# Building a graph's count matrix on TensorE: the register values of each step group moved from one row on partition 0 to a partition of their own

## The chip, the core and the metric

The kernel is one program on one core of a Trainium2 chip. Its time is the device time of that core in microseconds (us). TensorE (PE) multiplies, VectorE (DVE) and ScalarE (ACT) work on vectors, GpSimd (POOL) fills buffers and gathers, SyncE (SP) issues the plain DMAs here. Each engine has a sequencer of its own that also holds registers; a TENSOR_LOAD copies values of a tensor in the on-chip memory (SBUF, 128 partitions) into such registers, where they can be used as addresses.

## The reference

Four graph layers run one after the other on x (3125 nodes, 128 features), over the same 103,125 edges (`src`, `dst`, sorted by `dst`). The first two layers need plain sums over neighbours:

```python
edge_index = jnp.stack([src, dst])
h = jnp.maximum(_layernorm(x, axis=-1), 0.0)
x = x + _L0_gnn_ref(h, edge_index, ...)        # aggr = segment_sum(h[src], dst); batch norm
h = jnp.maximum(_layernorm(x, axis=-1), 0.0)
x = x + _L1_gnn_ref(h, ..., src, dst)          # two rounds of segment_sum(h[src], dst) / degree
h = jnp.maximum(_layernorm(x, axis=-1), 0.0)
x = x + _L2_gnn_ref(h, edge_index, ...)        # attention over the edges
h = jnp.maximum(_layernorm(x, axis=-1), 0.0)
x = x + _L3_gnn_ref(h, ..., edge_index, edge_type_8)   # a weight for each of 8 edge types, two rounds
return x
```

The change touches no number of this. It lies in a stage that prepares the three neighbour sums of the first two layers.

## The kernel before

**The count matrix.** The three sums are matrix products with a matrix that tells how often node s is a source of node d. The kernel builds it on the chip, in blocks of 4 target nodes: `CELLS` = 100 columns are one block (25 source tiles times 4 targets). The edges come in `STEPS` = 1596 steps, each 128 edges against one block. A step is one matmul (L670): a one-hot matrix of the low digit of `src` (`hot_lo`) times a one-hot matrix of the cell (`hot_cell`), added into the block's 100 columns in PSUM (`sums`).

**Epochs and windows.** 19 steps (`STEPS_OF`) form an epoch, of which there are 84 (`EPOCHS`). Two halves of PSUM take turns, one for each epoch. Four epochs form a window (21 of them), a buffer `filled[w % 2]` of 7700 columns (the trace calls it `adj_window`). Four engines work at each epoch, each in its own written order:

- DVE, `compare_epochs`: L647 writes `hot_lo`, L649 writes `hot_cell`; it may be one epoch ahead of TensorE (`estep_n`).
- TensorE, `count_edges`: L658 loads 20 registers (`SLOTS`), the places of the 19 steps in PSUM and one carry; L666 opens four banks with four matmuls of zeros; L670 is the 19 steps; L675 adds the columns that the last epoch left open; L679 closes the banks.
- ACT, `move_out`: L697 moves the half into the window buffer at a place that comes from a register (L685 loads four of them for a window).
- SP, `store_windows`: L704 loads one register, and L708 stores the whole window to DRAM (`adj`), 128 partitions of 30,800 bytes. It waits until the window's four epochs are moved out, and for the store before it.

**What a register load reads.** The values stand in `steprow`, [1, 84, 32] int32: all on partition 0, epoch e in 20 words from word 32 e. DVE makes them in L371 to L388; the mark of the last of these is `stepped`. All other loads of the program read partition 0 as well: `windowrow` (L704), `epochrow` (L685), `d0row` (L1066, 13 values), `pairrow` (L1194, 13), `pair_place` (L1386, 11 values from word 0, 11 and 22), `offrow` (L575, 13).

**The order around it.** TensorE's instructions run in the order in which they are written. Before its first load TensorE turns four weight matrices (L403) and waits for ACT to have taken them (L406). SP has issued the loads of the inputs and three stores of tables (L301 to L303) before the stage, and then waits for `stepped`. `mark` pairs such as `stepped` are a semaphore and the count to wait for; `Dma.did` adds 16 to its semaphore when a DMA has landed.

Of the kernel before, what the change touches and what calls it, by code (L numbers as in the profile page):

```python
# [6 lines left out]
I32 = mybir.dt.int32  # L7
# [5 lines left out]
ENG = mybir.EngineType  # L13
# [31 lines left out]
CELLS = HI * WD  # L45
KT = 7
STEPS_OF = 19
SLOTS = STEPS_OF + 1
EPOCHS = 84
# [4 lines left out]
SPANNED = GROUP * STEPS_OF + 1  # L54
# [54 lines left out]
def build(nc, a, out):  # L109
    with ExitStack() as ctx:  # L110
        def sem(name):
            return ctx.enter_context(nc.semaphore(name))
# [5 lines left out]
        A = Lane(nc.scalar, sem("s_act"))  # L118
        T = Lane(nc.tensor, sem("s_pe"))
# [83 lines left out]
        def tmp(stack, name, shape, dt=F32):  # L203
            return stack.enter_context(nc.sbuf_tensor(name, shape, dt))
# [5 lines left out]
        steprow = tmp(dense, "steprow", [1, EPOCHS, 32], I32)  # L210
# [163 lines left out]
        for q in (2, 3):  # L374
# [13 lines left out]
        stepped = V.did(V.after().tensor_tensor(carry[:, 1:WINDOWS, 0], b0w[:, 1:WINDOWS, 0], b0w[:, 0:WINDOWS - 1, 0],  # L388
                                                ALU.subtract))
# [243 lines left out]
        build = ExitStack()  # L633
# [8 lines left out]
        def compare_epochs():  # L642
            V.after()
            for e in range(EPOCHS):
                if e > 1:
                    nc.vector.wait_ge(estep_n, e - 1)
                nc.vector.tensor_tensor(hot_lo[e % 2][:, :, :], iota_lo[:, :, :],  # L647
                                        los[:, e, :].unsqueeze(1).to_broadcast([P, P, STEPS_OF]), ALU.is_equal)
                nc.vector.tensor_tensor(hot_cell[e % 2][:, :, :],  # L649
                                        iota_cell[:, :].unsqueeze(1).to_broadcast([P, STEPS_OF, CELLS]),  # L650
                                        cells[:, e, :].unsqueeze(2).to_broadcast([P, STEPS_OF, CELLS]),
                                        ALU.is_equal).then_inc(ehot_n, 1)

        def count_edges():
            T.need(stepped, A.now())
            for e in range(EPOCHS):
                half = sums[:, (e % 2) * 2048:(e % 2 + 1) * 2048]
                place = nc.values_load_multi_w_load_instructions(  # L658
                    steprow[0:1, e, 0:SLOTS], engines=(ENG.PE,), min_val=0, max_val=(SPANNED - 1) * CELLS,
                    skip_runtime_bounds_check_because="made on the chip from counts")[1]  # L660
                place = [nc.s_assert_within(v, 0, 2048 - CELLS, skip_runtime_bounds_check_because="made on the chip")
                         for v in place[:STEPS_OF]] + [place[STEPS_OF]]
                if e > 1:
                    nc.tensor.wait_ge(eout_n, e - 1)
                for j in range(4):
                    nc.tensor.matmul(half[:, j * 512:j * 512 + SLOTS // 4 * CELLS], zeros[:, 0:P],  # L666
                                     zeros[:, 0:SLOTS // 4 * CELLS], start=True, stop=False)
                nc.tensor.wait_ge(ehot_n, e + 1)
                for k in range(STEPS_OF):
                    m = nc.tensor.matmul(half[:, bass.ds(place[k], CELLS)], hot_lo[e % 2][:, :, k], hot_cell[e % 2][:, k, :],  # L670
                                         start=False, stop=False)
                m.then_inc(estep_n, 1)
                if e:
                    nc.tensor.wait_ge(eout_n, e)
                    nc.tensor.matmul(half[:, 0:CELLS], ident[:, :],  # L675
                                     filled[(e - 1) // GROUP % 2][:, bass.ds(place[STEPS_OF], CELLS)],
                                     start=False, stop=False)
                for j in range(4):
                    m = nc.tensor.matmul(half[:, j * 512:j * 512 + 1], zeros[:, 0:P], zeros[:, 0:1], start=False, stop=True)  # L679
                m.then_inc(ebuilt_n, 1)  # L680
# [20 lines left out]
        def store_windows():  # L701
            nc.sync.wait_ge(*stepped)
            for w in range(WINDOWS):
# [3 lines left out]
                    nc.sync.wait_ge(s_adj, 16 * w)  # L707
                nc.sync.dma_start(adj[:, bass.ds(first, SPANNED * CELLS)], filled[w % 2][:, :]).then_inc(s_adj, 16)  # L708

        compare_epochs()  # L710
        count_edges()
        move_out()
        store_windows()
# [848 lines left out]
```

## Time and profile before

| | |
|---|---|
| median of 3 runs | 5118.82 us (5105.4 to 5121.59) |
| the profiled execution | 5124.63 us, its span 5123.3 us |
| TensorE busy (matmuls) | 2855.5 us, 56% |
| VectorE busy | 1971.1 us, 38% |
| ScalarE busy | 677.7 us, 13% |
| GpSimd busy | 2395.5 us, 47% |
| the stage that the change touches | 84.0 to 503.6 us of the span |

The shares of busy time are means over stages that differ much: the build of the count matrix is the first tenth, the attention runs from about 1040 to 2600 us, and the rest is the last layer. The profile does not count register loads as busy time: where TensorE's sequencer is in one, the matmul array shows as idle and the wait is put down to "issue". How long each load took is seen when its line is asked for.

### The profile page before, as it was taken

How to read it: one execution, taken by the hardware profiler on the slowest of the kernel's cores; microseconds unless marked ns; L12 is line 12 of the kernel's file. 1: busy time of each engine (PE TensorE's matmuls, PEld its weight loads, DVE VectorE, ACT ScalarE, POOL GpSimd, SP SyncE). 2: the span in 40 equal slices, each digit the busy share in tenths (PEclk: the TensorE clock that was granted, in tenths of full speed). 3: DMA queues.
4: the chain of work that ended last, by engine and by line, in shares of the span. 5: the costliest groups of instructions: out<-in, count | busy, mean ns of one | idle time of the engine just before them, and what ended most of it. 6: DMA issues, size and time to landing. Idle time of an engine off the chain costs nothing.

```text
span 5123.3 us, 41736 instructions
## 1 busy us (share of the span) xinstructions
PE 2855.5 (56%) x12033; PEld 2017.8 (39%) x12033; DVE 1971.1 (38%) x3965; ACT 677.7 (13%) x1897; POOL 2395.5 (47%) x2466
## 2 busy tenths in 40 slices
PE   4666889946666656656626444444346444444343
PEld 3555445534444444444523333333333333333333
DVE  7676765655555555555562111111112111111111
ACT  2334010012222222222311000000001000000000
POOL 3000000055545555555313666666663666666665
PEclk8787989967777777777757555555557555555555
DMA  3444735444333443343304111111114111111111
GB/s 117 201 190 209 306 151 224 188 126 118 109 110 107 118 112 109 114 114 109 85 2 132 47 47 45 46 46 47 46 48 127 46 47 46 47 48 46 46 46 49
DMA packets 294311, 508.93 MB, mean 99 GB/s; under 512 B 68232, under 2 KB 239610, under 8 KB 288968
## 3 DMA queue, kind: packets, MB, share of 16 engines
q1 hardware_dynamic: 216304, 344.29, 18.9%
q0 software_dynamic: 77792, 161.98, 11.4%
q8 instruction: 110, 1.80, 0.1%
q14 instruction: 105, 0.86, 0.1%
HBM read 389.30 MB, written 116.74 MB: 99 GB/s over the span
## 4 chain that ended last, share of the span: by engine, by line
PE 37%; another core or an unknown queue 23%; issue 20%; DVE 6%; POOL 5%; ACT 5%; DMA 2%; ACTq 0%; DVEq 0%; SPq 0%; POOLq 0%
PE sums L587 9%; PE sums L748 8%; POOL edge_buffers L559 5%; PE sums L1105 3%; PE sums L1163 3%; PE sums L1108 3%; ACT trio L1185 3%; PE sums L670 3%; DVE edge_buffers L570 2%; PE sums L1119 2%; PE sums L666 2%; DMA edge_buffers<-rel_t,relidx 2%; PE sums L1477 2%; ACT adj_window L697 1%
## 5 line engine op out<-in xcount | busy, mean ns | idle before, releaser
L559 POOL DMA_INDIRECT edge_buffers<-rel_t,relidx x1612 | 1530.0, 949 | 888.1 <-issue 368.4
L587 PE MATMUL sums<-edge_buffers 128*128 128x128 f32 x3224 | 963.4, 432 | 1332.2 <-issue 1000.8
L587 PEld LDWEIGHTS sums<-edge_buffers 128*128 128x128 f32 x3224 | 748.0, 308 | 1548.9 <-issue 1547.3
L1061 POOL DMA_INDIRECT round_buffers<-xs_t,srcs x806 | 801.5, 994 | 1008.0 <-DVE round_buffers L1240 454.2
L570 DVE TENSOR_SCALAR edge_buffers<-iota,rel 128x128 f32<-128x128 f32 x1612 | 335.5, 300 | 1961.0 <-remote 1506.3
L1163 PE MATMUL sums<-round_buffers 128*128 128x128 f32 x1612 | 282.1, 321 | 441.5 <-ACT trio L1185 363.7
L1163 PEld LDWEIGHTS sums<-round_buffers 128*128 128x128 f32 x1612 | 236.1, 221 | 475.1 <-ACT trio L1185 390.5
L748 PE MATMUL sums<-adj_chunk,H 128*128 128x448 f32 x1050 | 400.2, 542 | 15.6 <-issue 14.4
L1231 DVE TENSOR_TENSOR positive<-positive,sums 128x384 f32<-128x384 f32 x310 | 154.2, 497 | 539.4 <-ACT positive L1175 504.8
L1108 PEld LDWEIGHTS sums<-round_buffers 128*128 128x128 f32 x1612 | 298.0, 238 | 99.5 <-issue 84.2
L1105 PE MATMUL sums<-round_buffers,ident 128*128 128x408 f32 x620 | 317.0, 601 | 28.9 <-DVE trio L1292 24.9
L613 ACT ACTIVATE trio<-sums,c_L_b 128x128 f32<-128x128 f32 x16 | 6.6, 412 | 2312.0 <-PE sums L543 2312.0
L1185 ACT ACTIVATE trio<-sums 128x128 f32 x806 | 225.8, 280 | 589.5 <-remote 319.3
L1108 PE MATMUL sums<-round_buffers 128*128 128x136 f32 x1612 | 296.7, 327 | 0.0
L893 POOL IOTA trio<- 128x806 int32 x1 | 0.8, 805 | 613.0 <-ACT H L502 613.0
L748 PEld LDWEIGHTS sums<-adj_chunk,H 128*128 128x128 f32 x1050 | 200.1, 191 | 210.4 <-issue 208.6
L697 ACT ACTIVATE adj_window<-sums 128x2000 f32 x84 | 154.4, 1838 | 265.3 <-PE sums L679 258.5
L666 PE MATMUL sums<-zeros 128*128 128x500 f16 x336 | 112.6, 470 | 131.8 <-issue 125.8
L649 DVE TENSOR_TENSOR hot_cell<-iota_cell,edge_cell 128x1900 f16<-128x1900 f16 x84 | 178.9, 2130 | 0.0
L1105 PEld LDWEIGHTS sums<-round_buffers,ident 128*128 128x128 f32 x620 | 124.7, 248 | 122.7 <-issue 116.0
L647 DVE TENSOR_TENSOR hot_lo<-iota_lo,edge_lo 128x2432 f16<-128x2432 f16 x84 | 125.3, 1491 | 118.3 <-PE sums L670 118.2
L1234 DVE TENSOR_REDUCE logits<-positive 128x24 f32<-128x384 f32 x310 | 155.3, 501 | 10.7
(273 smaller groups left out, 2683.4 us busy)
## 6 DMA issues: line engine op xcount, KB each, us to landing
adj_chunk<-adj SPq DMA_DIRECT2D x19, 5600.0 KB, 15.9
adj<-adj_window SPq DMA_DIRECT2D x21, 3850.0 KB, 11.2
round_buffers<-xd_t SPq DMA_DIRECT2D x806, 68.0 KB
round_buffers<-rel_tile SPq DMA_DIRECT2D x62, 832.0 KB
edge_buffers<-rel_t,relidx POOLq DMA_INDIRECT x1612
rel_t<-edge_buffers SPq DMA_DIRECT2D x50, 512.0 KB, 3.8
round_buffers<-xs_t,srcs POOLq DMA_INDIRECT x806
round_flags<-seg_tile SPq DMA_DIRECT2D x62, 26.0 KB
```

Source lines behind the costliest of these rows:

```text
L559: nc.gpsimd.indirect_dma_start(slot(t), None, table[:, :], bass.IndirectOffsetOnAxis(ap=index[:, t:t + 1], axis=0)).then_inc(slot_sem(t), 16)
L570: made = nc.vector.tensor_scalar(round_hots(i)[:, k, :], iota[:, :], rel[:, t:t + 1], None, ALU.is_equal)
L587: nc.tensor.matmul(sums[:, bass.ds(place[k], P)], slot(t), round_hots(i)[:, k, :], start=False, stop=False).then_inc(summed_n, 1)
L649: nc.vector.tensor_tensor(hot_cell[e % 2][:, :, :], iota_cell[:, :].unsqueeze(1).to_broadcast([P, STEPS_OF, CELLS]), cells[:, e, :].unsque ...
L666: nc.tensor.matmul(half[:, j * 512:j * 512 + SLOTS // 4 * CELLS], zeros[:, 0:P], zeros[:, 0:SLOTS // 4 * CELLS], start=True, stop=False)
L697: nc.scalar.activation(filled[w % 2][:, bass.ds(at[g], SLOTS * CELLS)].rearrange("p (a c) -> p a c", a=4), bank[:, (e % 2) * 4:(e % 2) * 4 ...
L748: m = nc.tensor.matmul(ps.rearrange("p (b w) -> p b w", w=WD), tables[:, hi, :], held[b][:, :, hi, :], start=(hi == 0), stop=(hi == HI - 1))
L1061: nc.gpsimd.indirect_dma_start(rows[r % RING][:, k * RW:(k + 1) * RW], None, xs_t[:, :], bass.IndirectOffsetOnAxis(ap=srcs[:, t:t + 1], ax ...
L1105: nc.tensor.matmul(pb[2 + q % 2][:, 0:(hi - lo) * RW], ident[:, :], rows[r % RING][:, lo * RW:hi * RW], start=True, stop=False)
L1108: m = nc.tensor.matmul(pb[2 + q % 2][:, (k - lo) * RW:(k - lo + 1) * RW], hotT[:, k * P:(k + 1) * P], win[r % 2][:, k * RW:(k + 1) * RW], ...
L1163: m = nc.tensor.matmul(pb[6 + q % 2][:, (k - lo) * P:(k - lo + 1) * P], msg[:, k * P:(k + 1) * P], hot[r % 2][:, k * P:(k + 1) * P], start ...
L1185: nc.scalar.activation(pairs[:, bass.ds(at[k], P)], pb[6 + q % 2][:, (k - lo) * P:(k - lo + 1) * P], ACT.Copy).then_inc(out_n, 1)
```

## The change

A second tensor `steps_of_epoch` of [84, 20] int32 is allocated, with epoch e's 20 values on partition e. One DMA on SP's queue copies the 84 rows from partition 0 to the 84 partitions; SP waits for `stepped` before it. TensorE's first load waits for that DMA in place of `stepped`, and each L658 reads partition e of the new tensor. In the built program each row of the new tensor begins at byte 228,416 of its partition, and row e of `steprow` at byte 137,248 + 128 e; both are multiples of 16.

```diff
         def count_edges():
-            T.need(stepped, A.now())
+            T.need(s_steps.now(), A.now())
             for e in range(EPOCHS):
                 half = sums[:, (e % 2) * 2048:(e % 2 + 1) * 2048]
                 place = nc.values_load_multi_w_load_instructions(
-                    steprow[0:1, e, 0:SLOTS], engines=(ENG.PE,), min_val=0, max_val=(SPANNED - 1) * CELLS,
+                    steps_of_epoch[e:e + 1, :], engines=(ENG.PE,), min_val=0, max_val=(SPANNED - 1) * CELLS,
                     skip_runtime_bounds_check_because="made on the chip from counts")[1]
...
+        steps_of_epoch = tmp(build, "steps_of_epoch", [EPOCHS, SLOTS], I32)
+        s_steps = Dma(sem("s_steps_turned"))
+        nc.sync.wait_ge(*stepped)
+        s_steps.did(nc.sync.dma_start(steps_of_epoch[:, :], steprow[0:1, :, 0:SLOTS]))
         compare_epochs()
         count_edges()
         move_out()
```

On TensorE at the start of the stage (L403 turns the weights, L658 is the first epoch's load, L666 opens the banks), the order before is this:

```order
L403 MATMUL sums<-ident,trio 128x128 [waits s_dve,s_par,s_pool]
L403 MATMUL sums<-ident,trio 128x128 x3
L658 TENSOR_LOAD steprow [waits s_act,s_dve]
L666 MATMUL sums<-zeros 128x500 x4
L670 ISA [waits s_epoch_hots]
```

and now:

```order
L403 MATMUL sums<-ident,trio 128x128 [waits s_dve,s_par,s_pool]
L403 MATMUL sums<-ident,trio 128x128 x3
L658 TENSOR_LOAD steps_of_epoch [waits s_act,s_steps_turned]
L666 MATMUL sums<-zeros 128x500 x4
L670 ISA [waits s_epoch_hots]
```

Nothing moved: the load stands at its place with another source and another semaphore. The same holds for the 83 loads after it.

On SP between the stores of tables (L302, L303) and the first window (L704), with + for what is added (L713 is the new DMA's line in the changed kernel):

```order
 L302 DMA seg_tile<-trio 128x7x128
 L303 DMA seg_tile<-trio 128x7x384
+L713 DMA steps_of_epoch<-steprow 84x1x20
 L704 TENSOR_LOAD windowrow
 L704 ISA x2
```

One DMA stands ahead of the first window's register load; the rest of SP's order is as it was.

## Rows read from the trace of the kernel before

**Rows 1.** Windows: length; busy of PE, PEld, DVE, ACT, POOL; PEclk, DMA share, GB/s.

```profile
84.00:503.60 419.60, 285.98 (x2434) 221.78 (x2434) 299.83 (x198) 154.51 (x85) 12.93 (x2) 0.80 0.45 189
503.60:5123.30 4619.70, 2540.43 (x9455) 1780.60 (x9455) 1609.30 (x3709) 513.33 (x1801) 2353.30 (x2440) 0.66 0.29 91
```

**Rows 2.** Line L658: duration in ns, min/median/max, then its first and last start.

```profile
L658 PEldq TENSOR_LOAD <-steprow x84: 1356/1372/4841, 84.0 to 496.8; - x84
```

**Rows 3.** The same line in 84:104, 104:111, 111:116, 116:124, 484.5:499.

```profile
L658 PEldq TENSOR_LOAD <-steprow x5: 1359/1367/1553, 84.0 to 100.7; - x5
...
L658 PEldq TENSOR_LOAD <-steprow x1: 4361/4361/4361, 104.5 to 104.5; - x1
...
L658 PEldq TENSOR_LOAD <-steprow x1: 2414/2414/2414, 111.7 to 111.7; - x1
...
L658 PEldq TENSOR_LOAD <-steprow x2: 1356/1356/1357, 116.7 to 120.7; - x2
...
L658 PEldq TENSOR_LOAD <-steprow x3: 1361/2267/4363, 484.9 to 496.8; - x3
```

**Rows 4.** Timeline of PE after the first store began: start, length, what, idle before.

```profile
104.79 0.24 PE L679 MATMUL sums<-zeros 128*128 128x1 f16 x4
108.94 1.82 PE L666 MATMUL sums<-zeros 128*128 128x500 f16 x4 [3.90 <-issue]
```

**Rows 5.** Windows between the starts of the loads of epochs 5 to 9.

```profile
104.56:111.74 7.18, 3.28 (x26) 2.16 (x26) 3.54 (x2) 1.84 (x1) 0.00 (x0) 0.68 0.97 412
111.74:116.74 5.00, 3.77 (x30) 2.65 (x28) 3.54 (x2) 1.84 (x1) 0.00 (x0) 0.50 0.25 102
116.74:120.75 4.01, 3.81 (x41) 3.31 (x38) 3.15 (x2) 1.84 (x1) 0.00 (x0) 0.92 0.00 0
120.75:124.70 3.95, 3.04 (x31) 2.44 (x30) 3.84 (x3) 1.84 (x1) 0.00 (x0) 1.00 0.29 125
```

**Rows 6.** DMA in 103:113.4 us, packets and the store's time to landing.

```profile
DMA packets 128, 3.94 MB, mean 379 GB/s; under 512 B 0, under 2 KB 0, under 8 KB 0
...
adj<-adj_window SPq DMA_DIRECT2D x1, 3850.0 KB, 11.3
```

**Rows 7.** Windows: three slices of the store, columns as in rows 1.

```profile
104.30:105.45 1.15, 0.73 (x9) 0.64 (x8) 0.85 (x2) 0.25 (x1) 0.00 (x0) 1.00 1.01 429
...
110.05:111.20 1.15, 1.15 (x10) 0.81 (x9) 0.00 (x0) 0.00 (x0) 0.00 (x0) 0.50 1.00 429
111.20:112.35 1.15, 1.15 (x15) 1.15 (x14) 0.00 (x0) 0.00 (x0) 0.00 (x0) 0.50 1.07 455
```

**Rows 8.** Other register loads, each line over the whole span.

```profile
L704 SPq TENSOR_LOAD <-windowrow x21: 262/273/712, 63.2 to 483.9; - x21
...
L575 PEldq TENSOR_LOAD <-offrow x124: 1092/1102/3470, 2742.8 to 5086.1; - x124
...
L1066 SPq TENSOR_LOAD <-d0row x62: 1181/1193/1246, 1037.2 to 2500.9; - x62
...
L1194 ACTq TENSOR_LOAD <-pairrow x62: 996/1013/1112, 1096.2 to 2553.2; - x62
...
L1386 PEldq TENSOR_LOAD <-pair_place x3: 1332/2647/2648, 2590.8 to 2620.2; - x3
```

**Rows 9.** Timeline of DVE, and L704 in 60:70 us, around the new DMA's place.

```profile
62.95 0.18 DVE L388 TENSOR_TENSOR steprow<-epoch_block 1x20 int32<-1x20 f32 x1
...
L704 SPq TENSOR_LOAD <-windowrow x1: 481/481/481, 63.2 to 63.2; - x1
```

**Rows 10.** DMA in 0:90 us: small issues, KB each, us to landing.

```profile
rel<-in_dst_col SPq DMA_DIRECT2D x1, 403.0 KB, 7.6
...
c_L_b_rel<-in_L_gnn_b_rel SPq DMA_DIRECT2D x1, 0.5 KB, 3.5
```

**Rows 11.** The two DVE lines of the stage.

```profile
L647 DVE TENSOR_TENSOR hot_lo<-iota_lo,edge_lo x84: 1480/1493/1496, 81.8 to 492.7; 128x2432 f16<-128x2432 f16 x84
...
L649 DVE TENSOR_TENSOR hot_cell<-iota_cell,edge_cell x84: 2127/2130/2134, 83.2 to 494.2; 128x1900 f16<-128x1900 f16 x84
```

## The prediction

> **What bounds the kernel now.** I read the windows first: the change can act only between 84.0 and 503.6 us, 419.6 us of the span; what comes after starts when the stage is done, so what is won or lost there goes into the end time one for one [rows 1]. Neither DVE (299.8 us busy of 419.6) nor ACT (154.5) fills the stage. Next the load line itself: 84 loads of 20 registers, median 1.372 us, but up to 4.841 [rows 2]. Asked for in slices it shows a pattern with a period of four epochs: about 1.36 us as a rule, 4.361 us for the load at 104.5, 2.414 us for the next, then 1.356 again [rows 3]. It repeats in each of the 20 windows that have a store beside them, down to the last, with 4.363 and 2.267 us: 40 of the 84 loads are over 1.6 us. The reader is to see that this is exactly when SP's store of a window is under way: it is issued at 103.4 and its 128 packets, 3.94 MB, land 11.3 us later [rows 6].
>
> The loads lie on the path. In the first slow one TensorE's array ends its work at about 105.0 and idles 3.90 us with the reason "issue" [rows 4]. The distances between four successive loads are 7.18, 5.00, 4.01 and 3.95 us [rows 5]; the first two exceed the last two by about 3.2 and 1.0 us, as their loads do by 3.00 and 1.06. So the sequencer of TensorE sets the pace: the load, then about 2.6 us of everything else. The clock does not enter: 5.00 - 2.41 = 2.59 us at a granted clock of 0.50 (the level of 1.2 GHz), and 3.95 - 1.36 = 2.59 at 1.00. DVE is close behind, with 1.493 + 2.130 = 3.62 us an epoch [rows 11], which is still under the shortest distance.
>
> **What the change could take away.** The excess of one window's loads over the quiet value is (4.361 - 1.357) + (2.414 - 1.357) = 4.06 us; times 20 windows it is 81 us [rows 3]. That is the whole prize, 1.6% of the kernel. Whether it is won hangs on one question: is it partition 0 that is slow to answer during a store, or any partition?
>
> The store treats all partitions alike: 128 packets, one for each partition's 30,800 bytes (3850 KB / 128), and no others [rows 6]. It moves 429 to 455 GB/s with the DMA engines busy all the time, in the first eighth as in the seventh [rows 7]. With 16 engines that is 27 GB/s each and 1.15 us a packet, so an engine has 8 packets in 9.2 us. Partition 0's own packet is thus in motion for one eighth of the store. But the load at 104.5 is slow for all of its 4.36 us, and the one at 111.7, in the seventh and eighth eighth, is slow again. What is busy for partition 0 is therefore not its own row; it is something that it shares with at least the eight rows of one engine, or with all 128. Since all 16 engines are busy to the end, each other partition shares an equally busy thing.
>
> The Trainium skill, "SBUF — State Buffer", section "Door 1: The DMA port swizzle", gives this a shape: 16 ports for the DMA side, each with eight partitions (0 to 3 and 32 to 35 on the first), and a transfer over 128 partitions reaches all of them. By that rule this change spreads the loads over ports that the same store fills alike, and the gain is nothing; by the opposite reading it would be the 81 us above. No row tells which partitions an engine serves; that the rate stays at 27 GB/s an engine agrees with the rule.
>
> I take the gain as 0. Its bounds are 0 (nothing of the wait goes) and -81 us (all goes).
>
> **What the load itself costs on another partition.** No row shows a load from any partition but 0, so I bound it by the other loads [rows 8]. 13 values take 1.102 us on TensorE, 20 take 1.357 (rows 3), one value on SP takes 0.273. This is no price for each value: 1.102 / 4 = 0.276 and 1.357 / 5 = 0.271 fit if up to four values that start at a multiple of four words go together (13 = 3 fours and 1, 20 = 5 fours). The 11 values of `pair_place` fit as well: from word 0 they take 1.332 us (2 fours and 3 singles, 0.266 each), from words 11 and 22 they take 2.647, 11 singles of 0.241. The new rows begin at a multiple of 16 bytes, so they remain 5 requests of 0.271. What may differ is the way to the partition. The same partition 0 costs ACT 1.013 / 4 = 0.253 and SP 1.193 / 4 = 0.298 a request: places of requesters differ by 0.045 us. If places of partitions differ as much, the 84 x 5 = 420 requests cost between -19 and +19 us; I take 0, since the epochs go through 84 partitions and near and far should cancel.
>
> During a store a request costs 4.361 / 5 = 0.872 us. About 7 requests in a window meet it (5 and some 2 of the next load), 140 in all; a difference of 0.06 us either way between partitions is 8 us, inside the same bounds.
>
> **What the change adds.** One DMA of 84 rows of 80 bytes on SP. Its source is ready at 63.1, when DVE's last write ends, and SP is idle there: its next instruction starts at 63.2 [rows 9]. The nearest small DMA lands after 3.5 us, the slowest of the first 90 us after 7.6 [rows 10]; so the rows are there at 67 to 72 us. TensorE does not ask before 84.0 [rows 2], when ACT has let it go. Cover of 12 us or more, cost 0; with the cover gone it would be at most 7.6 us once. Behind it on SP stands the first window's register load, delayed by the issue, about 0.4 us; the store that needs it comes at 103.4. Nobody waits. DVE, ACT and POOL have the same instructions as before, and the loads' count and place on TensorE are unchanged.
>
> **The sum.** 0 (wait) + 0 (price of a request) + 0 (the DMA) on the profiled execution's 5124.6 us. That one lies 5.8 us above the median of the runs, 5118.8; what is compared are medians, so I forecast 5119 us.
>
> **The rivals.**
>
> First, the wait belongs to partition 0. Then all 84 loads take 1.36 us, the windows last 4 x 4.0 us in place of 20.1, and the kernel takes 5119 - 81 = 5038 us. DVE's 3.62 us an epoch would not stop it, and a store (11.3 us) still fits into a window of 16 us. For it: every slow load in the trace does read partition 0, SP's too (0.712 against 0.273) and the last layer's (3.470 against 1.102) [rows 8], so nothing measured speaks for another partition. Against it: the argument of the eighths. A half of it is possible: partitions whose engine's share is done earlier, or which are reached past a less busy place, would bring 20 to 40 us, 5080 to 5099.
>
> Second, the other side: partitions away from 0 answer later. The mechanism is the trip of each request, 420 times in series. It decides from 15.4 / 420 = 0.037 us a request on; at the spread of 0.045 that the requesters show it is +19 us, 5138. A worse form is that the loads fall apart into single values, as from `pair_place`: 20 x 0.241 = 4.81 us, 3.46 more for each of 84 epochs, +290 us, 5409. Against this form stands the alignment of the rows.
>
> Third, the DMA lands late and the first load waits: at most +8 us, within no change.
>
> **How the numbers follow.** Below 0.3% (15.4 us) a measurement of this kernel can't be told from no change; the three runs of before already span 16 us. No change within that: 0.66 (the third rival in it). Faster: 0.19, 0.10 of it for the full 5038 and 0.09 for a part. Slower: 0.15, 0.12 for the trip and 0.03 for the single values. The range from 5070 to 5145 holds the middle case, most of the trip and most of the partial gains, and leaves out the full gain and the single values. The likeliest case alone has 5104 to 5134.
>
> **What would show it.** In the changed profile L658 should have 84 loads with the same two kinds: median about 1.37 us, and in each window one of about 4.3 and one of about 2.4 us. The stage should last from 84.0 to about 503 us, and TensorE's idle time before L666 by "issue" should remain. If the loads beside a store fall to 1.36 us, the first rival holds and the stage ends near 423. If the quiet loads leave 1.357 us and follow the partition number, it is the second. A first load that starts after 84.5 us would mean that the DMA is seen. I am wrong above all if the place where requests and the store meet is the partition, or a path that only the low partitions use.

## The result, and the profile after

The changed kernel takes 5135.6 us (median of 20 runs, 5113.6 to 5148.0) against 5122.1 us of the kernel before (20 runs): a ratio of 1.0024, 95% interval 1.0013 to 1.0035. Run once more beside other kernels it had 1.0014 (1.0005 to 1.0023). The middle of it, 0.24%, is inside the 0.3% that I called no change, though the interval reaches 0.35% and leaves out 0: the kernel did become a little slower. The forecast of 5119 us in 5070 to 5145 held. The profiled execution took 5140.6 us, its span 5139.3.

The load line L658 in the whole changed kernel, then in the slices that answer to [rows 3] (epochs 0 to 4, 5, 6 and 7; durations in ns as min/median/max, then first and last start in us):

```profile
L658 PEldq TENSOR_LOAD <-steps_of_epoch x84: 1357/1482/5502, 83.0 to 500.5; - x84
...
L658 PEldq TENSOR_LOAD <-steps_of_epoch x5: 1357/1366/1554, 83.0 to 99.7; - x5
...
L658 PEldq TENSOR_LOAD <-steps_of_epoch x1: 4405/4405/4405, 103.5 to 103.5; - x1
...
L658 PEldq TENSOR_LOAD <-steps_of_epoch x1: 2377/2377/2377, 110.7 to 110.7; - x1
...
L658 PEldq TENSOR_LOAD <-steps_of_epoch x1: 1362/1362/1362, 115.7 to 115.7; - x1
```

Up to here it is the kernel before: both slow loads of a window are there. But the median has gone from 1.372 to 1.482 us and the largest from 4.841 to 5.502. Later windows of the same kernel show why. These are the loads of epochs 29, 30, 31, then 33, 34, 35, then 65, 66, 67; the epoch's number is its partition:

```profile
L658 PEldq TENSOR_LOAD <-steps_of_epoch x1: 5285/5285/5285, 225.8 to 225.8; - x1
...
L658 PEldq TENSOR_LOAD <-steps_of_epoch x1: 1748/1748/1748, 233.8 to 233.8; - x1
...
L658 PEldq TENSOR_LOAD <-steps_of_epoch x1: 1426/1426/1426, 238.0 to 238.0; - x1
...
L658 PEldq TENSOR_LOAD <-steps_of_epoch x1: 4402/4402/4402, 246.2 to 246.2; - x1
...
L658 PEldq TENSOR_LOAD <-steps_of_epoch x1: 2311/2311/2311, 253.2 to 253.2; - x1
...
L658 PEldq TENSOR_LOAD <-steps_of_epoch x1: 1361/1361/1361, 258.1 to 258.1; - x1
...
L658 PEldq TENSOR_LOAD <-steps_of_epoch x1: 4197/4197/4197, 408.5 to 408.5; - x1
...
L658 PEldq TENSOR_LOAD <-steps_of_epoch x1: 2342/2342/2342, 415.4 to 415.4; - x1
...
L658 PEldq TENSOR_LOAD <-steps_of_epoch x1: 1359/1359/1359, 420.2 to 420.2; - x1
```

The price follows the partition, and starts anew at 32 and at 64. A quiet load takes 1.357 to 1.362 us on partitions 3 to 7, as it does on partition 0, then 1.38 to 1.39 on 8 to 19, 1.39 to 1.41 on 20 to 23, 1.41 to 1.43 on 24 to 31, and 1.36 again on 32. (Epochs 0 to 2 take 1.55, 1.38 and 1.37 us here, and the same in the kernel before, on partition 0. One load is out of line, the first from partition 64: 1.538 us, and 1.536 when the kernel ran again. No run explains it.) Beside a store the first load takes 4.2 to 4.6 us on partitions 0 to 15 of such a row of 32, and 5.2 to 5.5 on 16 to 31 (4.8 on 81). Summed over the 84 loads it is 199.9 us against 195.2; of the 4.7 us, 3.3 fall to the 40 loads beside a store and 1.4 to the other 44.

That is the stage's loss, too. From the first load's start to the last's it took 412.8 us before (84.0 to 496.8, [rows 2]) and 417.5 us now (83.0 to 500.5): 4.7 us of loads, 4.7 us of stage. The other 11 us of the difference between the two profiles lie behind the last load (12.3 us more there, less the 1.0 us by which the first load came earlier), in stages whose code is the same; the experiments bear on them.

The new DMA is out of sight, as seen in the rows of its line and of SP's next load (their counterpart is [rows 9]): it is issued at 62.5, its last packet has ended by 64.6, and the first load asks at 83.0.

```profile
L713 SPq DMA_DIRECT2D steps_of_epoch<-steprow x1: 967/967/967, 62.5 to 62.5; - x1
...
L704 SPq TENSOR_LOAD <-windowrow x1: 908/908/908, 63.5 to 63.5; - x1
```

### The profile page after: what moved, and what is told of

Its sections match the earlier page's. It is cut to its first block, busy times and chain, and to the rows that moved or that the text cites. A ratio compares the mean times of both kernels' runs of the same rounds, so it can differ in the third digit from the quotient of the medians.

```text
span 5139.3 us, 41737 instructions
## 1 busy us (share of the span) xinstructions
PE 2871.9 (56%) x12033; PEld 2027.3 (39%) x12033; DVE 1972.6 (38%) x3965; ACT 676.7 (13%) x1897; POOL 2392.3 (47%) x2466
## 4 chain that ended last, share of the span: by engine, by line
PE 36%; another core or an unknown queue 24%; issue 19%; POOL 6%; DVE 6%; ACT 5%; DMA 3%; ACTq 0%; SPq 0%; DVEq 0%; POOLq 0%
PE sums L752 8%; PE sums L587 7%; POOL edge_buffers L559 6%; PE sums L1109 3%; PE sums L1112 3%; PE sums L1167 3%; ACT trio L1189 3%; PE sums L670 3%; DVE edge_buffers L570 2%; DMA edge_buffers<-rel_t,relidx 2%; PE sums L1123 2%; PE sums L666 2%; PE sums L1481 1%; ACT adj_window L697 1%
## 5 line engine op out<-in xcount | busy, mean ns | idle before, releaser
L1167 PEld LDWEIGHTS sums<-round_buffers 128*128 128x128 f32 x1612 | 239.5, 224 | 468.5 <-ACT trio L1189 380.3
L1112 PEld LDWEIGHTS sums<-round_buffers 128*128 128x128 f32 x1612 | 305.0, 243 | 101.7 <-issue 83.2
L666 PE MATMUL sums<-zeros 128*128 128x500 f16 x336 | 114.4, 476 | 135.5 <-issue 132.3
L670 PEld LDWEIGHTS sums<-hot_cell,hot_lo 128*128 128x128 f16 x1596 | 148.2, 152 | 30.2 <-issue 19.8
```

Source lines behind the costliest of these rows:

```text
L1112: m = nc.tensor.matmul(pb[2 + q % 2][:, (k - lo) * RW:(k - lo + 1) * RW], hotT[:, k * P:(k + 1) * P], win[r % 2][:, k * RW:(k + 1) * RW], ...
L1167: m = nc.tensor.matmul(pb[6 + q % 2][:, (k - lo) * P:(k - lo + 1) * P], msg[:, k * P:(k + 1) * P], hot[r % 2][:, k * P:(k + 1) * P], start ...
```

## The experiments

A stage below is the time from the first load's start to the last one's in the profiled execution; the kernel before has 412.8 us. Eight of the kernels (hardly any store, the six with a part of the store, and the last) ran on two other chips, on which the kernel before takes 4393 us in place of 5123. The stage can be compared all the same: less the sum of its loads it lasts 217.1 to 217.8 us in all twelve profiles with one load before each epoch, whatever the chip (412.8 - 195.2 = 217.6 before).

**The changed kernel again.** No edit.

> The changed kernel once more, unaltered. In its first profile the stage of the count matrix, from the first to the last of the 84 loads, took 417.5 us against 412.8 before, and the rest of the 16 us stood in later stages. If the loads are the whole cause, the stage takes 417 to 418 us again, the later stages scatter around those of before, and the median is some 5 us above before. If the change does something to later stages, their excess of 9 to 11 us is there again and the median is some 13 us above before.

Measured: stage 417.6 us, median 5131.8 against 5123.6 of the kernel before beside it, +8 us (+3 to +12 by the interval). The 4.7 us of the stage are there again to 0.1 us. The attention stage, whose 1563.1 us made most of the rest in the first profile (1553.6 before), took 1551.2 us this time: that excess did not come back.

**The copy made, but not used.**

> The changed kernel with its new DMA and its new wait, but with the loads reading the old row on partition 0; the copy is not used. If the place of the values is the cause, the stage is back at 412 to 413 us, with loads beside a store at 4.3 and 2.4 us, and the median is within 3 us of before. If the DMA, the wait or the shifted program is the cause, the median stays some 13 us above before.

Against the changed kernel:

```diff
-                    steps_of_epoch[e:e + 1, :], engines=(ENG.PE,), ...
+                    steprow[0:1, e, 0:SLOTS], engines=(ENG.PE,), ...
```

Measured: stage 412.3 us, ratio to before 0.9997 (0.9988 to 1.0006). Its loads are the old ones:

```profile
L658 PEldq TENSOR_LOAD <-steprow x84: 1355/1372/4402, 84.4 to 496.7; - x84
```

The DMA, the wait on it and one more instruction on SP cost nothing that can be measured. What the change costs comes from where the loads read: between this kernel and the changed one measured beside it, which differ in nothing else, lie 5.3 us of stage and 8.5 us of median. The attention stage took 1542.6 us here. In four profiles, with the same code, it has spread over 20 us, so single profiles can't tell whether the change reaches it.

**All rows on partition 28.** `steprow` gets all 128 partitions, the DMA copies to partition 28, the loads read there.

> All 84 rows on partition 28, one of the group whose loads were slowest in the changed kernel (quiet 1.425, beside a store 5.3 and 1.75 us). If the partition's place sets the price of a request, every quiet load takes 1.42 to 1.43 us and every first load beside a store 5.2 to 5.5, and the stage grows by 5 to 12 us against 412.8. If it was something else that changed with the epoch number, the loads go on from 1.357 to 1.425 with the epoch, or all stay at 1.357, and the stage is as before or as in the changed kernel.

```diff
-                    steprow[0:1, e, 0:SLOTS], engines=(ENG.PE,), ...
+                    steprow[ROWS_ON:ROWS_ON + 1, e, 0:SLOTS], engines=(ENG.PE,), ...
...
+        ROWS_ON = 28
...
+        s_steps.did(nc.sync.dma_start(steprow[ROWS_ON:ROWS_ON + 1, :, 0:SLOTS], steprow[0:1, :, 0:SLOTS]))
```

```profile
L658 PEldq TENSOR_LOAD <-steprow x84: 1422/1436/5403, 84.5 to 506.7; - x84
```

No load is below 1.422 us now, whatever the epoch. Beside a store the first takes 5.28 to 5.40 us, the second 1.6 to 2.0 (2.25 once). Stage 422.2 us, 9.4 above before; ratio 1.0018 (1.0009 to 1.0027). The place of the partition is the cause of the stage's loss, and the dose fits: twice the loss of the changed kernel, in which only a part of the epochs lies that far. The loads sum to 9.5 us more: 2.9 in the 44 quiet ones, at 0.069 us each, and 6.6 in the 40 beside a store. The row has the layout that it has in the kernel before, so the layout of the new tensor is not the cause.

**Hardly any store.** Of each window 100 of 7700 columns are stored in the stage; the excerpt leaves out the lines that fill the rest afterwards.

> Leaves out nearly all of each window's store (100 of 7700 columns are written during the stage; the rest of the matrix in DRAM is filled afterwards with the content of a window buffer, so the total time is not comparable, only the stage). Rows on partition 0. If the store's reading of SBUF is what slows the loads, all 84 take 1.36 to 1.4 us and the stage is 81 us shorter, near 332 us. If they are slowed by something else of the window's change (ACT, the semaphores), a load of 4 us remains in each window.

```diff
-                nc.sync.dma_start(adj[:, bass.ds(first, SPANNED * CELLS)], filled[w % 2][:, :]).then_inc(s_adj, 16)
+                nc.sync.dma_start(adj[:, bass.ds(first, CELLS)], filled[w % 2][:, 0:CELLS]).then_inc(s_adj, 16)
```

```profile
L658 PEldq TENSOR_LOAD <-steprow x84: 1356/1359/1556, 82.9 to 414.7; - x84
```

Stage 331.8 us: 81.0 us less, the 81 us that the prediction worked out as the prize, and the loads sum to 80.8 us less. Every slow load is the store's doing, and each microsecond of it is on the path.

**A part of the store, six ways.** Each window's store moves one half of the partitions, or 16 of them; the rows are on partition 0, 64 or 28. The rest of the matrix is filled after the stage, so only the stage and its loads say something.

> Each window's store moves partitions 64 to 127 only (the other half is filled after the stage, with other content; only the stage is comparable). The loads read partition 0. If a request waits at the port of its own group of partitions, the loads are quiet, 1.36 to 1.4 us, though a store of half the bytes is under way, and the stage is near 332 us. If it waits on a path that all DMA reads share, the loads beside the store are slow, from 2 to 4.4 us.

> The counterpart: each window's store moves partitions 0 to 63 only, loads from partition 0, the other half filled after the stage. By the port theory the port of partition 0 is read throughout the store: loads of about 4.3 us as before. By the shared path they are as slow as in the kernel that stores partitions 64 to 127.

> Store of partitions 64 to 127 only, and the rows on partition 64, which the store reads (other half filled after the stage). By the port theory the loads are slow again, about 4.2 us and 2.3 us as in the changed kernel for epochs 65 and 66, though partition 0 was quiet under the same store. By the shared path there is no difference from the kernel with the rows on partition 0.

> Each window's store moves partitions 16 to 31 only (0.49 MB, some 4.6 us; the rest of the matrix is filled after the stage with other content, so only the stage is comparable). Rows on partition 0. The halves showed that a request is slowed also by a store of the half in which its partition doesn't lie (5.2 us for 5 requests against 6.4). If what is shared there is something near the partition (0 and 64 belong together), a store of 16 to 31 leaves the loads quiet at 1.36 to 1.4 us. If it is a path that all requests and all DMA reads share, the load beside the store is still slow, above 2 us.

> The same store of partitions 16 to 31, with the rows on partition 28, which it reads. By the theory of the near place: slow, over 4 us for as long as the store lasts, while partition 0 stayed quiet. By the shared path: not much different from the rows on partition 0 (at most the fifth by which the two halves differed).

> The counterpart on the other side: store of partitions 0 to 15, rows on partition 0. By the near place: slow like the rows on 28 under the store of 16 to 31. By the shared path: the same in all three kernels.

The edit of the first of the six; the others differ in the partitions named. The lines that fill the rest are left out again:

```diff
-                nc.sync.dma_start(adj[:, bass.ds(first, SPANNED * CELLS)], filled[w % 2][:, :]).then_inc(s_adj, 16)
+                nc.sync.dma_start(adj[64:128, bass.ds(first, SPANNED * CELLS)], filled[w % 2][64:128, :]).then_inc(s_adj, 16)
```

The load line in the order of the six above; the third of the three durations is the slowest load:

```profile
L658 PEldq TENSOR_LOAD <-steprow x84: 1357/1364/5300, 84.7 to 509.5; - x84
```
```profile
L658 PEldq TENSOR_LOAD <-steprow x84: 1355/1374/6401, 83.3 to 518.0; - x84
```
```profile
L658 PEldq TENSOR_LOAD <-steprow x84: 1356/1365/6397, 85.0 to 520.0; - x84
```
```profile
L658 PEldq TENSOR_LOAD <-steprow x84: 1356/1361/4455, 83.8 to 476.4; - x84
```
```profile
L658 PEldq TENSOR_LOAD <-steprow x84: 1422/1426/5559, 84.2 to 494.4; - x84
```
```profile
L658 PEldq TENSOR_LOAD <-steprow x84: 1357/1361/5127, 83.6 to 488.2; - x84
```

The landing of a store of 64 partitions, and of 16:

```profile
adj<-adj_window SPq DMA_DIRECT2D x5, 1925.0 KB, 11.3
```
```profile
adj<-adj_window SPq DMA_DIRECT2D x6, 481.2 KB, 6.1
```

| store of | rows on | first load beside it, us (20 windows) | stage, us |
|---|---|---|---|
| all 128 | 0 | 4.3 to 4.4 (others: 3.4, 4.0, 4.8) | 412.8 |
| 64 to 127 | 0 | 5.2 to 5.3 | 424.7 |
| 0 to 63 | 0 | 6.3 to 6.4 | 434.7 |
| 64 to 127 | 64 | 6.3 to 6.4 (one 4.6) | 434.9 |
| 16 to 31 | 0 | 4.4 to 4.5 (one 3.8) | 392.6 |
| 16 to 31 | 28 | 4.9 to 5.2 (one 5.6) | 410.2 |
| 0 to 15 | 0 | 4.9 to 5.1 (one 4.6) | 404.7 |

In no window is the first load beside a store quiet, in whichever partitions the store reads. In the fourth kernel the store reads partitions 16 to 31 only, and the load from partition 0 still waits until that store is through: it takes 4.38 to 4.46 us (3.75 once), and the last of the store's 16 packets ends 4.3 to 4.7 us after the load's start. So the wait is above all on something that every request shares with the store. That the request's own partitions are read adds to it: 1.1 us in 6.4 for the halves, with the rows on 0 and with the rows on 64, and 0.6 in 5.0 for the stores of 0 to 15 and of 16 to 31 with the rows on 0. My port theory, in which partition 0 stays quiet there, falls.

Half the bytes took the same time to land, 11.3 us, and yet the requests were slower than beside the whole store, 1.06 and 1.28 us each against 0.872. The price does not follow the rate. That the DMA engines queue up at fewer places and hold the common path while they do would explain it; this is argued, not shown. What the shared thing is stays open as well.

**Loads moved away from the store.** TensorE loads the second epoch's values with the first's, before the store moves.

> The kernel before, with the values on partition 0, but the load of the second epoch of each window is made together with that of the first (40 registers, just before the store begins); the third and fourth stand as they did. If only the time matters that TensorE's sequencer spends in requests while a store is under way, one load a window (4.36 us) meets the store in place of one and a half, and about 1.06 us a window goes: stage 412.8 - 21 = 392 us, median some 20 us below before. If the wait is passed on (each load is slow again because the store now lies beside the next ones), the stage stays at 412.

```diff
+            LOADED_AT, places = {0: 2, 2: 1, 3: 1}, {}
             for e in range(EPOCHS):
...
+                for n in range(e, e + LOADED_AT.get(e % GROUP, 0)):
+                    places[n] = nc.values_load_multi_w_load_instructions(steprow[0:1, n, 0:SLOTS], ...)[1]
+                place = places.pop(e)
```

Its load line, and who waited in 84 to 470 us (us in total, times, longest):

```profile
L660 PEldq TENSOR_LOAD <-steprow x84: 1356/1360/4817, 83.4 to 482.2; - x84
```
```profile
PE sums L669 <- ACT adj_window L700: 49.6, 21, 2.8
```

Stage 398.8 us, ratio 0.997 (0.9958 to 0.9982): faster than both kernels, by 12 us in the median and 15 by the ratio, in place of the 20 expected. The loads gave back what was expected or more, 171.2 us in all against 195.2, but the stage only 14 of these 24 us.

The 49.6 us "for ACT" are not what took the other 10. A wait is put down to the semaphore that came last, and here TensorE's sequencer was in its two loads meanwhile. In the fifth window:

```profile
L660 PEldq TENSOR_LOAD <-steprow x2: 1357/1358/1358, 158.0 to 159.4; - x2
...
158.61 1.84 ACT L700 ACTIVATE adj_window<-sums 128x2000 f32 x1 [1.74 <-PE sums L682]
...
160.87 1.73 PE L669 MATMUL sums<-zeros 128*128 128x500 f16 x4 [2.37 <-ACT adj_window L700]
```

ACT was done at 160.45, the second load at 160.8, and L669 began at 160.87: it waited for the load. The 10 us lie behind that, in the two epochs that now follow each other without a load. With the gap between the two loads they take 5.74 us in the mean, where two epochs took 5.27 without their loads before: 0.47 us more in each of 21 windows, which makes the 10. The matmul L678 of the second epoch adds columns that ACT has moved out of the first, and in 20 of the 21 windows its instruction runs 0.04 us after ACT's move has ended (0.11 in the other). So the pair lasts as long as the first epoch on the array, 2.95 to 4.06 us, then ACT's 1.84 us and 0.3 us around it. With a load between the epochs that move was covered by the load. The first of these terms follows TensorE's granted clock. Here are a pair at the level of 1.2 GHz (0.51) and two at 2.4 GHz (1.00), columns as in [rows 1]:

```profile
315.38:321.59 6.21, 6.18 (x43) 4.10 (x44) 3.68 (x3) 1.84 (x1) 0.00 (x0) 0.51 0.93 397
141.56:146.88 5.32, 5.28 (x53) 4.38 (x53) 3.68 (x3) 1.84 (x1) 0.00 (x0) 1.00 0.96 403
431.75:436.94 5.19, 5.15 (x53) 4.29 (x53) 3.58 (x3) 1.84 (x1) 0.00 (x0) 1.00 0.89 380
```

At the full clock the pair takes what it took before, 5.2 to 5.3 us. That the clock does not enter, as the prediction read it, holds only as long as a load follows each epoch.

**52 values ahead.** The first epoch of a window loads also 12 values of the third.

> The kernel before with the values on partition 0, but at the first epoch of each window TensorE loads 52 values (its own 20, the next epoch's 20 and 12 of the third's: 13 requests, 3.5 us, just before the store's data moves); the third epoch loads its last 8 values, the fourth its 20. With a slow request 0.6 us above a quiet one, 2 requests meet the store in place of 5: stage 399 - 20 x 1.8 = 363 us where the kernel with the loads 2, 1, 1 had 398.8 and the kernel before 412.8; a few us more if the fourth epoch's load now begins before the store has ended. Median some 45 us below before. If the wait is passed on, the stage stays near 399.

```diff
+            AHEAD, places = 12, {}
+            LOADED_AT = {0: ((0, 0, SLOTS), (1, 0, SLOTS), (2, 0, AHEAD)), 2: ((0, AHEAD, SLOTS),), 3: ((0, 0, SLOTS),)}
...
```

The load line over its stage, then the first loads of 20 and 12 values and the first of 8:

```profile
L661 PEldq TENSOR_LOAD <-steprow x105: 597/1358/2006, 83.6 to 467.1; - x105
...
L661 PEldq TENSOR_LOAD <-steprow x2: 852/1114/1377, 85.2 to 86.7; - x2
...
L661 PEldq TENSOR_LOAD <-steprow x1: 597/597/597, 93.2 to 93.2; - x1
```

The loads of 4 us are gone, the longest is 2.006 us; what still meets the store is the load of 8 values, 1.73 to 2.01 us there against 0.597 quiet. Stage 383.5 us, ratio 0.9931 (0.9917 to 0.9944) on a chip where the kernel before takes 4392.8 us: 31 us. The expectations of 363 us and of some 45 us of median were missed, for the same reason as in the last kernel: the loads sum to 146.1 us, 49 less than before, and the stage gives 29. The pair of epochs without a load takes 6.18 us in the mean, gaps between the loads included, 0.91 more than before in each of 21 windows, which makes 19 of the missing 20 us. In all 21 the second epoch's instruction comes 0.04 us after the end of ACT's move, so again it is the first epoch on the array and then ACT; DVE's 3.62 us an epoch [rows 11] is not what it waits for. No pair had the full clock here: the first epoch took 3.5 to 4.1 us.

## Why the prediction was right

**The stage and its pace: right.** That loads lie on the path one for one was the base of the whole sum; 4.7 us of load for 4.7 us of stage, and 80.8 for 81.0 us in the kernel with hardly any store, show it.

**"Is it partition 0 that is slow to answer, or any partition?": right, any.** The argument of the eighths held, and the first rival is refuted by the changed profile itself: on each of the 20 partitions that meet the start of a store, 5 to 81, the load takes 4.2 us or more. It left open whether the shared thing is a group of eight rows or all 128. I leaned on the first, with the rule of the Trainium skill, "SBUF — State Buffer", section "Door 1: The DMA port swizzle". By that rule partitions 0 to 63 reach 8 of the 16 ports and 64 to 127 the other 8. The half stores agree with it: their 64 partitions take the 11.3 us of 128. But that is not where the register loads wait for the most part, as the store of 16 to 31 shows. Both readings gave a gain of 0, so the sum did not suffer from it.

**The price of a request on another partition: the bound held, the value was off.** I took 0 within +/-19 us, "since near and far should cancel". They don't: partition 0 is at the cheap end, and the others are as cheap or dearer, by up to 0.014 us a request when quiet (1.426 against 1.357 us for 5). The term measures +4.7 us, 1.4 in quiet loads and 3.3 beside stores. With a bound on both sides of 0 I had not asked whether the starting point is a middling one. And the spread of the requesters, from which the bound came, says nothing of partitions: that it held is luck. By the sign that the prediction names, quiet loads that leave 1.357 us and follow the partition number, this is the second rival, the trip of a request, in a small dose; its point of decision, 0.037 us a request, was not reached. The sign of "the same two kinds" of load failed too: the median went to 1.482 us, and on partitions 16 to 31 of each 32 the slow loads are 5.3 and about 1.7 us. The form with single values did not occur: aligned rows stay at five requests.

**The DMA: right, 0.** The copy that is made but not used has a ratio of 0.9997.

**What stays open.** The stage explains 4.7 us, 0.09%. The second measurement (0.05 to 0.23%) holds that; the first (0.13 to 0.35%) does not. Over both, the 31 runs of the changed kernel have a mean 10.7 us above the 48 of the kernel before, with a 95% interval of 3.4 us to either side, so about 6 us are more than noise and lie outside the stage. The kernel with all rows on partition 28 has no such rest: its mean is 8.6 us above, and its stage gives 9.4. Nothing in the profiles tells what the rest is, and the prediction has no term for it. That the total stayed within 0.3% is therefore in part luck.

## What to carry to other kernels

A register load from SBUF is, by its price of 0.254 us for each four values, a chain of requests one after the other on the issuing sequencer; if that sequencer sets the pace, move the loads in time, away from big stores out of SBUF, rather than in place. Spreading data over partitions helps only what waits for a partition; before doing it, ask whether the wait lasts while the other side is busy elsewhere. And when loads are taken from between two pieces of work, work out first what they covered: here ACT's move, and the array at the lower clock, took 10 of 24 us, and 20 of 49. A wait that the profile puts down to a semaphore is first to be checked against the register loads, which it doesn't count.

## What the runs showed of the hardware

- A load of 20, 12 and 8 aligned values takes 1.357, 0.852 and 0.597 us on TensorE's sequencer. An estimate from these: 0.088 us and 0.254 for each four values.
- The answer's time depends on the partition, from 1.357 us (0 to 7) to 1.426 us (28 to 31) for 20 values, and the course repeats from 32 and from 64 on, as far as partition 83.
- Beside a store out of SBUF such a load takes 4.2 to 6.4 us as a rule, even where the store reads 16 other partitions only. The 62 loads of L1066, in the attention stage, whose DMAs mostly write SBUF, took 1.246 us at most [rows 8]; but there the DMA engines were busy 0.38 of the time, against 0.97 beside the first slow load [rows 5], so a load beside writes at the full rate was not seen.
- An epoch on TensorE's array, from the end of its load to the end of its last matmul, took 2.95 to 3.16 us at a granted clock of 1.00 and 4.06 at 0.51 (the kernel with loads moved away from the store).
- TensorE's sequencer can hold 52 loaded values at once: the kernel with 52 values ahead ran.
